# Row additions of a mixture-of-experts kernel: one chain of 512 columns or two of 256, and when the loads go out

## What is computed

```
probs = softmax(x @ router_weight); the 8 best experts of each row, weights normed to 1
xe    = rows of x gathered by expert, 256 slots each (what is over is dropped)
h     = silu(xe @ gate_proj) * (xe @ up_proj)          # 512 -> 192
ye    = h @ down_proj                                  # 192 -> 512
out   = x;  out[row] += weight * ye[slot]              # 8 additions to a row, by 8 experts
```

## Time and profile before

| | us |
|---|---|
| median of 3 runs (1781.33 to 1793.82) | 1786.95 |
| profiled execution | 1788.09 |
| its span | 1785.9 |

### The profile page before, as it was taken

How to read it: one execution, slowest core, us unless ns; L and a number is a source line. 1 busy time by engine, 2 the same in 40 slices (tenths; PEclk the granted TensorE clock), 3 DMA queues, 4 the chain that set the end, 5 groups by cost and what they waited for, 6 DMA issues and landing times.

```text
span 1785.9 us, 25234 instructions
## 1 busy us (share of the span) xinstructions
PE 1572.3 (88%) x8016; PEld 1004.1 (56%) x8016; DVE 1253.0 (70%) x2994; ACT 973.9 (55%) x1938; POOL 796.8 (45%) x889
## 2 busy tenths in 40 slices
PE   5899999989999999999999889616999999999994
PEld 2444455444454454454444444215999887888883
DVE  2477778767768767777777677235888777787782
ACT  3455675655665665665655644313666555565562
POOL 4122326444464564563554445653444333334343
PEclk8889999999999999999999999857999999999997
DMA  9957654453463363352333222026999999999995
GB/s 329 299 168 248 225 143 127 141 180 109 129 211 105 120 197 92 105 156 86 94 92 94 79 59 64 25 82 231 268 289 256 267 259 259 263 263 266 274 250 81
DMA packets 150387, 311.91 MB, mean 175 GB/s; under 512 B 27674, under 2 KB 37786, under 8 KB 150256
## 3 DMA queue, kind: packets, MB, share of 16 engines
q1 hardware_dynamic: 111344, 238.89, 40.0%
q0 software_dynamic: 38912, 71.43, 20.1%
HBM read 141.25 MB, written 155.91 MB: 166 GB/s over the span
## 4 chain that ended last, share of the span: by engine, by line
PE 51%; DMA 14%; DVE 10%; issue 7%; POOL 5%; another core or an unknown queue 4%; SPq 4%; ACT 3%; DVEq 1%; POOLq 0%; ACTq 0%
DMA out_rows<-y_slots,row_ids 12%; PE bank L693 7%; PE bank L705 5%; PE bank L684 5%; POOL out_rows L1526 4%; PE bank L662 3%; PE bank L727 3%; PE bank L607 2%; DVE max_col L1202 2%; PE bank L613 2%; PE bank L802 2%; SPq L489 2%; PE bank L804 2%; PE bank L803 2%
## 5 line engine op out<-in xcount | busy, mean ns | idle before, releaser
L1202 DVE TENSOR_REDUCE max_col<-bank 128x1 f32<-128x512 f32 x512 | 340.7, 683 | 169.2 <-PE bank L684 145.9
L966 ACT ACTIVATE p_t<-bank 128x512 f32<-128x512 f32 x512 | 294.4, 596 | 212.5 <-PE bank L693 189.3
L1526 POOL DMA_INDIRECT out_rows<-y_slots,row_ids x128 | 212.7, 1662 | 344.9 <-DMA out_rows<-y_slots,row_ids 250.2
L1484 POOL DMA_INDIRECT slot_rows<-row,slot_i x256 | 255.2, 997 | 77.5 <-issue 76.6
L693 PE MATMUL bank<-q_stack,k_stack 98*128 98x512 f32 x512 | 277.8, 545 | 6.0 <-ACT p_t L966 4.1
L1472 POOL TENSOR_TENSOR p_sum<-p_t 128x512 f32<-128x512 f32 x128 | 168.4, 1322 | 206.5 <-ACT p_t L966 203.2
L684 PE MATMUL bank<-k_stack,q_stack 96*128 96x512 f32 x512 | 214.0, 419 | 4.6 <-DVE max_col L1202 4.2
L693 PEld LDWEIGHTS bank<-q_stack,k_stack 98*128 98x128 f32 x512 | 98.1, 193 | 192.6 <-issue 166.4
L802 PE MATMUL bank<-gate_up_hi,x_slots_t_hi 128*128 128x384 f32 x512 | 184.4, 360 | 2.8 <-DVE x_slots_t_lo L1330 2.6
L804 PE MATMUL bank<-gate_up_hi,x_slots_t_lo 128*128 128x384 f32 x512 | 173.0, 338 | 0.0
L803 PE MATMUL bank<-gate_up_lo,x_slots_t_hi 128*128 128x384 f32 x512 | 172.9, 338 | 0.0
(11 more groups left out here) (186 smaller groups left out, 3298.3 us busy)
## 6 DMA issues: line engine op xcount, KB each, us to landing
gate_up<-in_gate_up SPq DMA_DIRECT2D x64, 768.0 KB
slot_rows<-row SPq DMA_DIRECT2D x64, 577.0 KB, 7.9
x_slots<-slot_rows SPq DMA_DIRECT2D x64, 577.0 KB, 5.5
k_stack<-prob SPq DMA_DIRECT2D x192, 128.0 KB, 3.8
down<-in_down SPq DMA_DIRECT2D x64, 384.0 KB
q_stack<-x_t SPq DMA_DIRECT2D x128, 128.0 KB
x<-in_x SPq DMA_DIRECT2D x16, 512.0 KB, 3.3
ctx<-in_ctx SPq DMA_DIRECT2D x16, 512.0 KB, 4.3
```

The lines of the kernel that those rows point to most:

```text
L966: e.activation(p_t[step % 2][:, h, :], psum[n % 2][:, :], ACT.Exp, scale=SCALE).then_inc(free[n % 2], 1)
L1202: e.tensor_reduce(max_col[quad % 2][:, h, c:c + 1], psum[2 + n % 2][:, :], X, ALU.max, negate=True).then_inc(free[2 + n % 2], 1)
L1484: e.indirect_dma_start(out=slots_dram, in_=rows[b % 2][:, k, :], in_offset=None, out_offset=bass.IndirectOffsetOnAxis(ap=slot_i[b % 2][:, ...
L1526: e.indirect_dma_start(out=out, out_offset=bass.IndirectOffsetOnAxis(ap=row_ids[e_ % NI][:, q, :].bitcast(U32), axis=0), in_=ye[e_ % NY][: ...
```

## The change

Each addition of 128 rows of 512 columns becomes two of 256 columns. The output is seen as rows of 256 (`half_rows`), so that row numbers are doubled where they are made, and the second half has an offset of 256 elements. There is a chain for each half: part 0 of an expert waits only for part 0 of the expert before, part 1 for part 1. GpSimd issues part 0 of both units, then part 1 of both. `issue_mark` and `adds_issued` go, and SyncE no longer waits for them. There are four y buffers. All who waited for `added` now wait for both parts.

```diff
     NX = 4
     NB = 5
     NW = 3
-    NY = 3
+    NY = 4
     NI = 6
     ND = 3
     BC = NHEAD * C
@@ -263,8 +263,7 @@
         weights_of = [sem(f"expert_weights_in{i}") for i in range(NB)]
         down_of = [[sem(f"down_pair_in{i}_{k}") for k in range(2)] for i in range(ND)]
         rows_of = [sem(f"expert_rows_in{i}") for i in range(NB)]
-        adds_issued = sem("adds_issued")
-        added = [[sem(f"added{i}_{q}") for q in range(2)] for i in range(2)]
+        added = [[[sem(f"added{i}_{part}_{q}") for q in range(2)] for part in range(2)] for i in range(2)]
         xt_hi_ok = sem("xt_hi_ok")
         gu_hi_ok = sem("gu_hi_ok")
         gu_lo_ok = sem("gu_lo_ok")
@@ -386,7 +385,6 @@
         hid = [sb(f"hidden{i}", [P, 2 * P]) for i in range(2)]
         ht_hi, ht_lo = ([sb(f"hidden_t_{part}{i}", [P, 2, P], F32R) for i in range(2)] for part in ("hi", "lo"))
         ye = [sb(f"y_slots{i}", [P, 2, T]) for i in range(NY)]
-        issue_mark = sb("issue_mark", [P, 1])
         row_ids = [sb(f"row_ids{i}", [P, 2, 1], I32) for i in range(NI)]
 
 
@@ -549,14 +547,14 @@
             for e_ in range(NEXP):
 
 
-                w.wait_ge(adds_issued, e_ + 1)
                 if e_ + NB < NEXP:
                     load_rows(e_ + NB)
                 if e_ + NB + 2 < NEXP:
                     load_weights(e_ + NB + 2)
             for i in range(2):
-                for q in range(2):
-                    w.wait_ge(added[i][q], 16 * (NEXP // 2))
+                for part in range(2):
+                    for q in range(2):
+                        w.wait_ge(added[i][part][q], 16 * (NEXP // 2))
             w.wait_ge(slots_filled, 16 * (NEXP + 1))
 
         @block.tensor
@@ -1034,7 +1032,8 @@
                 e_, s = divmod(u, 2)
                 w.wait_ge(full[6 + u % 2], full_a[6 + u % 2] + u // 2 + 1)
                 if e_ >= NY:
-                    w.wait_ge(added[(e_ - NY) % 2][s], 16 * ((e_ - NY) // 2 + 1))
+                    w.wait_ge(added[(e_ - NY) % 2][0][s], 16 * ((e_ - NY) // 2 + 1))
+                    w.wait_ge(added[(e_ - NY) % 2][1][s], 16 * ((e_ - NY) // 2 + 1))
                 e.activation(ye[e_ % NY][:, s, :], psum[6 + u % 2][:, :], ACT.Copy,
                              scale=xe[e_ % NB][:, s, T + 1 + e_:T + 2 + e_]).then_inc(free[6 + u % 2], 1)
 
@@ -1240,7 +1239,7 @@
                         w.wait_ge(slots_filled, 16 * (NEXP + 1))
                     e.tensor_scalar(rw[:, k, 0:T], xb[:, k, :], row_mv4[:, k, 0:1], row_rstd4[:, k:k + 1], ALU.subtract,
                                     ALU.mult).then_inc(rows_ok, 1)
-                    e.tensor_scalar(rw[:, k, T:T + 1].bitcast(I32), row_no[:, 0:1], float((b * HALF + k) * P), None,
+                    e.tensor_scalar(rw[:, k, T:T + 1].bitcast(I32), row_no[:, 0:1], float(2 * (b * HALF + k) * P), None,
                                     ALU.add)
                 elif what == "peak":
                     bank, _ = filled("disp", "route", b)
@@ -1319,8 +1318,9 @@
                 i = e_ % NB
                 w.wait_ge(rows_of[i], 16 * (e_ // NB + 1))
                 if e_ >= NI:
-                    w.wait_ge(added[(e_ - NI) % 2][0], 16 * ((e_ - NI) // 2 + 1))
-                    w.wait_ge(added[(e_ - NI) % 2][1], 16 * ((e_ - NI) // 2 + 1))
+                    for part in range(2):
+                        for q in range(2):
+                            w.wait_ge(added[(e_ - NI) % 2][part][q], 16 * ((e_ - NI) // 2 + 1))
                 e.tensor_copy(row_ids[e_ % NI][:, :, :], xe[i][:, :, T:T + 1].bitcast(I32)).then_inc(row_ids_ok, 1)
 
             def turn(u):
@@ -1503,9 +1503,9 @@
             e.memset(fill_row[:, :, :], 0.0).then_inc(pool_step, 1)
             w.wait_ge(pool_step, step.up())
             for c in range(2):
-                e.iota(fill_row[:, c, T:T + 1].bitcast(I32), pattern=[[0, 1]], base=ROWS + c * P,
-                       channel_multiplier=1).then_inc(fill_ready, 1)
-            e.iota(row_no[:, :], pattern=[[P, 2]], base=0, channel_multiplier=1,
+                e.iota(fill_row[:, c, T:T + 1].bitcast(I32), pattern=[[0, 1]], base=2 * (ROWS + c * P),
+                       channel_multiplier=2).then_inc(fill_ready, 1)
+            e.iota(row_no[:, :], pattern=[[2 * P, 2]], base=0, channel_multiplier=2,
                    allow_small_or_imprecise_dtypes=True).then_inc(pool_ready, 1)
             for _, ev in gpsimd_order:
                 if ev[0] == "prep":
@@ -1515,23 +1515,23 @@
                 elif ev[0] == "disp":
                     dispatch(*ev[1:])
 
-            def add_rows(u):
-                e_, q = divmod(u, 2)
-                if q == 0:
-                    w.wait_ge(row_ids_ok, e_ + 1)
-                    if e_:
-                        w.wait_ge(added[(e_ - 1) % 2][0], 16 * ((e_ - 1) // 2 + 1))
-                        w.wait_ge(added[(e_ - 1) % 2][1], 16 * ((e_ - 1) // 2 + 1))
-                w.wait_ge(free[6 + q], full_a[6 + q] + e_ + 1)
-                e.indirect_dma_start(
-                    out=out, out_offset=bass.IndirectOffsetOnAxis(ap=row_ids[e_ % NI][:, q, :].bitcast(U32), axis=0),
-                    in_=ye[e_ % NY][:, q, :], in_offset=None, compute_op=ALU.add).then_inc(added[e_ % 2][q], 16)
-                if q == 1:
-                    w.wait_ge(adds_issued, e_)
-                    e.memset(issue_mark[:, :], 0.0).then_inc(adds_issued, 1)
-
-            for u in range(U):
-                add_rows(u)
+            half_rows = out.rearrange("r (k t) -> (r k) t", k=2)
+
+            def add_rows(e_, part):
+                w.wait_ge(row_ids_ok, e_ + 1)
+                if e_:
+                    w.wait_ge(added[(e_ - 1) % 2][part][0], 16 * ((e_ - 1) // 2 + 1))
+                    w.wait_ge(added[(e_ - 1) % 2][part][1], 16 * ((e_ - 1) // 2 + 1))
+                for q in range(2):
+                    w.wait_ge(free[6 + q], full_a[6 + q] + e_ + 1)
+                    e.indirect_dma_start(
+                        out=half_rows, in_=ye[e_ % NY][:, q, part * T // 2:(part + 1) * T // 2], in_offset=None,
+                        out_offset=bass.IndirectOffsetOnAxis(ap=row_ids[e_ % NI][:, q, :].bitcast(U32), axis=0),
+                        element_offset=part * T // 2, compute_op=ALU.add).then_inc(added[e_ % 2][part][q], 16)
+
+            for e_ in range(NEXP):
+                for part in range(2):
+                    add_rows(e_, part)
 
 
 def kernel(x, ctx_2048, L0_xattn_theta_w, L0_xattn_theta_b, L0_xattn_phi_w, L0_xattn_phi_b, L0_xattn_g_w,
```

## The result

| | before | after |
|---|---|---|
| median of 4 runs each, us | 1784.14 | 1867.32 |
| ratio, 95% interval | | 1.046 (1.035 to 1.057) |
| profiled span, us | 1785.9 | 1873.8 |

What follows compares the result with a forecast made beforehand. DMA engines were taken to bound the expert stage: 517 us of work packed at 0.99 takes 522 us, ending at 1758; 2 us for the last receipt gives 1760, plus 2.2 makes 1762 us. Range 1744 to 1818.

Steps and rivals of the forecast that it cites:

- (a): SyncE's loads no longer wait for the mark: they move forward about two experts, and TensorE's waits for slot rows go.
- does less than it says: Rival: additions still pace, y waits for buffers and loads for y, so loads come little earlier; within no change's 0.24.
- (d): Two addition chains: a half's loop of 7.76 us, less for half the bytes, is covered by GpSimd's own 7.85 us.
- no-change case: Rival: three quarters of start-ups stay, 31 us more work, or half-chain landings lengthen: 1793 us; chance 0.24.
- The DMA floor: Expert stage: 517 us of DMA engine work, packed at 0.99, takes 522 us; span 1760, the latest floor.
- The open term, start-ups: Additions' DMA start-up: four cost 1.96 us an expert, half covered, leaving 0.98 us, as much as before.
- The slower rival: DMA start-up is engine time however full the queue: 9.36 us of engines an expert, 1825 us; chance 0.19.
- (b): Removing the mark and its memset on GpSimd after the second issue: nothing on the path.
- (c): Four GpSimd issues per expert in place of two, 1,662 ns each plus 0.30 us between: 7.85 us an expert.
- floors of GpSimd and TensorE: Expert stage paced by GpSimd at 7.85 us an expert or TensorE at 7.80: span ends at 1743 or 1742.
- (f): Doubled row numbers and eight semaphores' waits at ScalarE and VectorE, met long before: nothing.
- (e): Four y buffers: ScalarE waits only 1.9 us for additions, so worth nothing alone; room when additions lag.

Runs made afterwards that it cites:

- e1: Kernel before without SyncE's wait for the mark, so loads go out once the buffer is free; full rows, three y buffers: ratio 1.071 to the kernel before.
- f4: Kernel before with weight loads cut to 64 words of each row from the eighth expert on: ratio 1.007 to the kernel before.
- f3: Changed kernel with weight loads cut to 64 words of each row from the eighth expert on: ratio 0.967 to the kernel before, loop 7.91 us.
- e3: Kernel before without SyncE's wait for the mark and with four y buffers in place of three, full rows: ratio 1.067 to the kernel before.
- e2: Changed kernel with the mark put back after an expert's fourth issue and SyncE waiting for it before loads: ratio 1.020 to the kernel before.
- g3: Kernel before, but SyncE waits for the landing of an expert's first addition in place of the mark: ratio 1.004 to the kernel before.
- f1: Kernel before, but SyncE waits for the mark of one expert earlier, so loads go out one expert sooner: ratio 1.006 to the kernel before.
- h1: Changed kernel with an expert's loads released in four pieces at four moments in place of all at once: ratio 1.012 to the kernel before.
- h2: Kernel before (full rows, three y buffers) with its loads in four pieces and no wait for the mark: ratio 1.042 to the kernel before.
- h0: The changed kernel run again, unchanged, in a later session: ratio 1.047 to the kernel before, expert stage 649 us.

## Why the prediction was wrong, by its own steps

The additions paced the kernel before from the start, and not only after 1390 us as I had it: its first 20 loops average 8.6 us.

**(a) Loads move forward, and "late in their place can only be a load that stands in a full queue": wrong, and this is the step that failed.** Late in their place were the additions. I had read that y waits for additions and loads wait for y, under the rival "does less than it says", and saw in it only loads that come no earlier. It also fixes the moment: the instant when the next addition is issued. e1 prices it at 7.1% alone, with full rows.

**(d) Two chains: wrong by the landing.** I took 5.5 us "less for half the bytes" and 0.30 us of wake-up. The fourth landing is 7.4, the wake-up 0.8, the loop 10.2 and not 7.76: the term that was mis-sized. The text's own end (7.2 us, loop 9.5, "the chain would rule again") was close, but I gave it no chance of its own beyond the no-change case.

**The DMA floor: wrong.** 517 us of packet time was taken for work that the engines must do. It contains waiting. The share fell to 0.85 while the kernel got slower, and with most of the weights cut away (f4) full rows stayed as slow. The floor could not carry the forecast, and a latency chain was the bound before as well: 1.93 + 5.9 + 0.84 = 8.7 us.

**The open term, start-ups: right in kind.** Four cost 3.76 us an expert with their data, two cost 3.87: the two more add nothing. The slower rival (1825, start-ups as engine time) has the right sign for a wrong reason. The receipt of the write, which that rival weighs, is short here: the last packet of the kernel before ends at 1784.57 us, and the landing stands at 1784.92; the first packets come only 2.45 us after an issue.

**(b), (c): right.** 256 issues at 1,636 ns against 1,660; the floors of GpSimd and TensorE nearly hold once most of the weight loads are away (f3: 7.91 us). **(f): nearly right;** VectorE's copy of the row numbers waits 14.1 us for additions, 13 times. **(e): nearly right**, e3 against e1 gives 12 us at most.

The rule of the Trainium skill that I weighed (DMA: Bandwidth & Descriptors, "Rules for kernel authors": coalesce small transfers) pointed the right way beside full loads: e2, with the mark back, loses 2.0%. With few weights the halves win 4% (f3 against f4), so it is no price of the halving as such. The 8 us that I estimated for packet overhead were too little. In the smooth part of an addition a row of 1,024 bytes takes 102 ns of an engine and one of 2,048 bytes 178 (medians): 512 x 0.102 / 16 = 3.26 us an expert against 2.85, 27 us over the stage. As the engines were not the floor, this is packet time and not loss.

What the old wait was: it kept the loads 1.7 us behind the second issue, where they run in the pause between two experts' additions. Around that place the time is nearly flat: g3, with loads 2.9 us later, and f1, an expert sooner at the same place, differ by 0.4% and 0.6%. At the landing that frees y it is 7%.

## What to carry to other kernels

A busy share of DMA engines need not be a floor, least of all when the packets are additions to HBM and their time holds waiting: add up one loop of the dependent chain, issue, first packet, last packet, landing, wake-up, and see whether it gives the period. Before a wait is removed, ask which event releases the transfers instead; if the same event also releases the critical DMA, the bulk loads go ahead of it. When a chain of small dependent DMAs shares engines with bulk loads, place the loads in the chain's pause. Finer chains close the pause; there spreading is the better of the two (h1 1.012, the burst 1.047), but where a pause was, spreading fills it (h2 1.042).

## What the runs showed of the hardware that was not expected

- Loads issued by SyncE within 1 us of an indirect addition by GpSimd reach the engines first: the addition's first packets come 4.6 and 5.5 us after its issue (e1, means of the two units) and not 2.5.
- A landing takes 0.84 us to GpSimd's next issue in nearly every loop, and an issue of 128 rows takes 1.54 us at the least, whether the rows are 1 KB or 2 KB.
- A row of 1,024 bytes added to HBM takes 102 ns of an engine where 2,048 bytes take 178: half the bytes cost 57% of the time.
- When TensorE stands still for a sixth of the time, its granted clock falls to 0.90 from 1390 to 1740, and the first of its gate/up products takes 394 ns and not 360; the clock is back at 0.99 when loads are spread (h1).
- On one chip the first addition came at 1235 to 1241 us in f1 to f4 and at 1150 in h0 to h2, in a later session, with the expert stage as long as ever (649 us in h0, 648 in the changed kernel's first profile). Times of different sessions are compared by ratios alone.
